# One maximum before the key normalisation in latent attention, the attentions' tables loaded a stage ahead, and unread products in the tails of two expert stages

## The reference

```python
x = x + jnp.tanh(g_xattn[0]) * _L0_xattn_ref(_layernorm(x), ctx, mask, ...)      # 16 heads of 8, mask added
x = x + jnp.tanh(g_ffn[0])   * _L0_ffn_ref(_layernorm(x), ...)                    # ternary weights
x = x + jnp.tanh(g_xattn[1]) * _L1_xattn_ref(_layernorm(x), ctx, ctx, ...)        # 16 heads, relative bias
x = x + jnp.tanh(g_ffn[1])   * _L1_ffn_ref(_layernorm(x), ...)                    # 64 experts, top 3, capacity 64
x = x + jnp.tanh(g_xattn[2]) * _L2_xattn_ref(ctx, _layernorm(x), ...)             # latent attention, below
x = x + jnp.tanh(g_ffn[2])   * _L2_ffn_ref(_layernorm(x), ...)                    # 8 experts, top 2
x = x + jnp.tanh(g_xattn[3]) * _L3_xattn_ref(_layernorm(x), ctx, ...)             # 16 heads, rotated
x = x + jnp.tanh(g_ffn[3])   * _L3_ffn_ref(_layernorm(x), ...)                    # 16 experts, top 2, and a shared one
```

```python
q = (ln @ Wq).reshape(b, m, h, d).transpose(0, 2, 1, 3)
kv = jnp.concatenate([xn @ Wkv, ln @ Wkv], axis=1)
...
qn = rmsnorm(q, qn_g) * scale
kn = rmsnorm(k, kn_g)
sim = jnp.einsum('bhid,bhjd->bhij', qn, kn)
...
attn = jax.nn.softmax(sim.astype(jnp.float32), axis=-1)
out = jnp.einsum('bhij,bhjd->bhid', attn, v)
return out.transpose(0, 2, 1, 3).reshape(b, m, h * d) @ Wout + bout
```

## Time and profile before

| | us |
|---|---|
| median of 3 runs | 1539.1 (1534.62 to 1541.3) |
| profiled execution | 1543.05 |
| its span, first to last instruction | 1541.2 |
| mean granted clock of PE in it | 0.932 |
| busy: PE, DVE, ACT, POOL | 1311.7, 832.4, 690.6, 504.9 |

### The profile page before, as it was taken

The page is one execution under the profiler, slowest core; times in us unless marked ns, Lnnn a source line. Parts: engine busy times, 40 slices in busy tenths (PEclk is TensorE's granted clock), DMA queues, the critical chain, the costliest instruction groups (busy, mean ns, idle before and its releaser), DMA issues. The chain is left out here.

```text
span 1541.2 us, 19784 instructions
## 1 busy us (share of the span) xinstructions
PE 1311.7 (85%) x7007; PEld 570.9 (37%) x7007; DVE 832.4 (54%) x1380; ACT 690.6 (45%) x1158; POOL 504.9 (33%) x479
## 2 busy tenths in 40 slices
PE   5878687649967899999999999999949966677998
PEld 2223232228962333333333333333336752222443
DVE  3767666372335666656665666566274334632554
ACT  3354434422225566656664666465334433353222
POOL 0012301056621555444444455354317750010000
PEclk9899889869987999999999999999979987797999
DMA  8600310149632000000000000000041132000340
GB/s 216 240 1 0 89 39 1 49 156 378 252 84 80 1 1 1 1 0 1 0 1 0 1 1 1 1 1 0 1 146 47 53 91 92 1 1 1 86 95 14
DMA packets 44268, 85.74 MB, mean 56 GB/s; under 512 B 7646, under 2 KB 27230, under 8 KB 43422
## 3 DMA queue, kind: packets, MB, share of 16 engines
q1 hardware_dynamic: 30124, 70.44, 14.3%
q0 software_dynamic: 4544, 9.32, 2.2%
q10 hardware_dynamic: 9504, 4.72, 1.1%
HBM read 76.56 MB, written 11.04 MB: 57 GB/s over the span
## 5 line engine op out<-in xcount | busy, mean ns | idle before, releaser
L2595 ACT ACTIVATE a_prob<-a_TP 128x512 f32<-128x512 f32 x256 | 138.9, 595 | 124.1 <-PE a_TP L2369 122.2
L2726 DVE TENSOR_REDUCE a_lat<-a_SP 128x2 f32<-128x1024 f32 x128 | 156.0, 1218 | 53.0 <-PE a_SP L2335 53.0
L2858 POOL TENSOR_TENSOR a_acc<-a_prob 128x512 f32<-128x512 f32 x64 | 79.8, 1267 | 275.8 <-ACT a_prob L2595 275.8
L2365 PE MATMUL a_TP<-a_qn,a_kn 64*128 64x512 f32 x512 | 148.4, 645 | 2.6 <-ACT a_prob L2595 2.6
L2381 PE MATMUL a_MS<-a_prob,a_V 128*64 128x512 f32 x512 | 123.9, 604 | 0.2 <-ACT a_prob L2595 0.2
L3342 DVE TENSOR_REDUCE a_nm<-a_A 128x8 bf16<-128x616 f32 x84 | 67.0, 797 | 53.4 <-PE a_A L3062 53.3
L3520 POOL TENSOR_TENSOR a_on<-a_osb,a_rden 128x512 f32<-128x512 f32 x9 | 11.4, 1272 | 247.0 <-ACT a_osb L3234 247.0
L2867 POOL TENSOR_TENSOR a_acc<-a_acc,a_prob 128x512 f32<-128x512 f32 x64 | 79.8, 1268 | 18.4 <-ACT a_prob L2595 18.4
L2862 POOL TENSOR_TENSOR a_acc<-a_acc,a_prob 77x512 f32<-77x512 f32 x64 | 80.2, 1273 | 0.0
L2365 PEld LDWEIGHTS a_TP<-a_qn,a_kn 64*128 64x128 f32 x512 | 40.5, 185 | 104.7 <-issue 76.5
L2369 PE MATMUL a_TP<-a_negm,onesb 64*128 64x512 bf16 (+1 forms) x320 | 65.1, 378 | 0.0
(11 more groups left out here) (525 smaller groups left out, 2859.0 us busy)
## 6 DMA issues: line engine op xcount, KB each, us to landing
ring_w<-in_F_w SPq DMA_DIRECT2D x64, 512.0 KB, 8.8
f_wide<-weight_rows SPq DMA_DIRECT2D x24, 256.0 KB, 5.6
a_maskT<-in_maskT SPq DMA_DIRECT2D x1, 2304.0 KB
a_biasT<-in_biasT SPq DMA_DIRECT2D x1, 2304.0 KB
f_b<-in_F_b SPq DMA_DIRECT2D x1, 2048.0 KB
token_rows<-f_xtok ACTq DMA_DIRECT2D x8, 256.0 KB, 7.9
a_biasQ<-in_biasQ SPq DMA_DIRECT2D x3, 616.0 KB, 6.5
ring_w<-expert_rows SPq DMA_DIRECT2D x6, 256.0 KB, 7.1
```

What stands on the lines that cost most here:

```text
L2365: nc.tensor.matmul(TP[0:n, h, :], keys(h), qn[half(h), r % 4, :], start=True, stop=False)
L2595: nc.scalar.activation(prob[0:n, 2 * k + h, :], TP[0:n, h, :], ACT.Exp, bias=rowneg[0:n, b:b + 1] if k == 0 else 0.0).then_inc(p_ready, 1)
L2726: nc.vector.tensor_reduce(lat[:, g % 2, 2 * u:2 * u + 2], SP[:, :, :], AX.X, ALU.max, negate=True).then_inc(s_used, 1)
L2858: nc.gpsimd.tensor_tensor(acc[:, h, :], prob[:, 2 + h, :], prob[:, 4 + h, :], ALU.add).then_inc(added, 1)
```

## The change

Four edits.

1. In `latent_attention`, DVE's `reduce(r + 2, 0)` stands before `norm_k(r + 3)` instead of behind it.
2. The tables of a0, a1 and a3 are placed and loaded by a class `QuadTables` outside the attention: a0's (with the mask) in the block of the shared loads, behind them on SP; a1's weights, vectors and key masks in f0's block; a3's in f2's first block, behind f2's own weights. a1's bias tables are still placed and loaded in a1's block, where they now stand first on SP. What each consumer waits for is unchanged.
3. In f1, 10 products of 128 x 512 that nobody reads are issued on PE behind the last expert product, and one more behind each batch's transposes.
4. In f2 the same with 8 and one for each batch.

```diff
@@ latent_attention, DVE
                     if r + 1 < R:
                         shift(r + 1)
+                    if r + 2 < R:
+                        reduce(r + 2, 0)
                     if r + 3 < R:
                         norm_k(r + 3)
-                    if r + 2 < R:
-                        reduce(r + 2, 0)
                     add_last(r)
@@ load_shared, SP, behind the shared loads
             sp.dma_start(c.ctxrep[:, :, :], d["ctxrep"]).then_inc(loaded, 16)
+            more_loads(sp)
             sp.wait_ge(x_in, 16)
             sp.wait_ge(loaded, 12 * 16)
@@ ternary_ffn
         with nc.Block() as block:
+            @block.sync
+            def _(sp):
+                more_loads(sp)
@@ sorted_glu_moe, PE
                     pe.wait_ge(wide_kept, NT)
                     pe.wait_ge(rest_kept, NT)
+                    def unread(count):
+                        for i in range(count):
+                            nc.tensor.matmul(VP[:, 0, :], c.center[:, :], c.xn[:, 0:S], start=True, stop=True)
+
+                    unread(8)
                     for b in range(B):
                         pe.wait_ge(summed, QT * (b + 1))
...
                         mm.then_inc(back, 1)
+                        unread(1)
@@ capacity_moe, PE
                     down(PAIRS - 1)
+                    unread(10)          # into IDLE, a bank that nothing reads
...
                         mm.then_inc(back, 1)
+                        unread(1)
@@ QuadTables (new), what SP issues
+    def load(self, sp):
+        for dst, src in self.first:
+            sp.dma_start(dst, src).then_inc(self.k_in, 16)
+        for dst, src in self.loads:
+            sp.dma_start(dst, src).then_inc(self.loaded, 16)
+
+    def load_mask(self, sp):
+        self.load(sp)
+        self.load_tall(sp, self.maskT, self.c.dram["maskT"])
+
+    def load_bias(self, sp):
+        for i in range(3):
+            sp.dma_start(self.biasQ[:, i, :], self.c.dram["biasQ"][:, i, :]).then_inc(self.bq_loaded[i], 16)
+        self.load_tall(sp, self.biasT, self.c.dram["biasT"])
@@ flamingo_kernel
+            with ExitStack() as until_first:
+                masked = QuadTables(c, until_first, "a0", "L0_Wq", "L0_Wk", "L0_Wv", mask=True)
+                load_shared(c, masked.load_mask)
+                quad_attention(c, "a0", 0, masked, bv=True, mask=True, more_loads=first_loads(c, ring, ternary))
+            with ExitStack() as until_second:
+                biased = QuadTables(c, until_second, "a1", "L1_Wq", "L1_Wk", "L1_Wv", wo="L1_Wo", relbias=True)
+                ternary_ffn(c, "f0", 4, ternary, biased.load)
+                quad_attention(c, "a1", 1, biased, bv=True, wo=True, relbias=True)
```

More of the change, by code:

```diff
@@ L2011, in _, with unread @@
                             down(n - 1)
+                    def unread(count):
+                        for i in range(count):
+                            nc.tensor.matmul(IDLE[:, :], c.center[:, :], c.xn[:, 0:S], start=True, stop=True)
                     down(PAIRS - 1)
+                    unread(10)
                     for b in range(B):
@@ L2907, in _, with __init__, sb, place_bias @@
                 pool.wait_ge(added, 6 * R)
-def quad_attention(c, name, gate, wq, wk, wv, bq=None, bk=None, bv=None, wo=None, bo=None,
-                   mask=False, relbias=False, rope=False, more_loads=None):
+class QuadTables:
+    def __init__(self, c, ctx, name, wq, wk, wv, wo=None, mask=False, relbias=False, rope=False):
+        self.c = c
+        nc, d = c.nc, c.dram
+        def sb(n, shape, dt=F32):
+            return ctx.enter_context(nc.sbuf_tensor(f"{name}_{n}", shape, dt))
+        self.Wq, self.Wk, self.Wv = sb("Wq", [P, P]), sb("Wk", [P, P]), sb("Wv", [P, P])
+        self.vec = sb("vec", [P, 8])
+        self.first = [(self.Wk[:, :], d[wk]), (self.vec[:, :], d[name + "_vec"])]
+        self.loads = [(self.Wq[:, :], d[wq]), (self.Wv[:, :], d[wv])]
+        if wo:
+            self.Wo = sb("Wo", [P, P])
+            self.loads.append((self.Wo[:, :], d[wo]))
+        if mask:
+            self.maskT = sb("maskT", [P, B * CH, S])
+            self.maskQ = sb("maskQ", [P, B * QT, SK])
+            self.loads.append((self.maskQ[:, :, :], d["maskQ"]))
+        if relbias:
+            self.keym = sb("keym", [P, B * SK], I32)
+            self.rowm = sb("rowm", [P, B * CH], I32)
+            self.first += [(self.keym[:, :], d["keymask"].partition_broadcast(P)),
+                           (self.rowm[0:CR, :], d["rowkeymask"])]
+        if rope:
+            self.Wqp, self.Wkp = sb("Wqp", [P, P]), sb("Wkp", [P, P])
+            self.blk8 = sb("blk8", [P, P])
+            self.qcs = sb("qcs", [P, 2, S])
+            self.kcs = sb("kcs", [P, 2, B * SK])
+            self.first += [(self.Wkp[:, :], d[wk + "_p"]), (self.blk8[:, :], d["blk8"]), (self.kcs[:, :, :], d["kcs"])]
+            self.loads += [(self.Wqp[:, :], d[wq + "_p"]), (self.qcs[:, :, :], d["qcs"])]
+        self.k_in, self.loaded, self.tall_in = (c.sem(f"{name}_{n}") for n in ("k_in", "loaded", "tall_in"))
+        self.bq_loaded = [c.sem(f"{name}_bq_loaded{i}") for i in range(3)] if relbias else []
+    def load(self, sp):
[3 more added lines that the diff above has]
+            sp.dma_start(dst, src).then_inc(self.loaded, 16)
+    def place_bias(self, ctx):
+        self.biasT = ctx.enter_context(self.c.nc.sbuf_tensor("a1_biasT", [P, QUAD * CH, S], F32))
+        self.biasQ = ctx.enter_context(self.c.nc.sbuf_tensor("a1_biasQ", [P, 3, QUAD * ROWS], F32))
+    def load_tall(self, sp, dst, src):
+        even = CR - CR % 16
+        sp.dma_start(dst[0:even, :, :], src[0:even, :, :]).then_inc(self.tall_in, 16)
+        sp.dma_start(dst[even:CR, :, :], src[even:CR, :, :]).then_inc(self.tall_in, 16)
+    def load_mask(self, sp):
[5 more added lines that the diff above has]
+        self.load_tall(sp, self.biasT, self.c.dram["biasT"])
@@ L2914, in quad_attention @@
+def quad_attention(c, name, gate, tables, bv=False, wo=False, mask=False, relbias=False, rope=False,
+                   more_loads=None):
     nc, d = c.nc, c.dram
@@ L2925, in quad_attention @@
         adds = mask or relbias
-        Wq, Wk, Wv = sb("Wq", [P, P]), sb("Wk", [P, P]), sb("Wv", [P, P])
-        vec = sb("vec", [P, 8])
+        Wq, Wk, Wv, vec = tables.Wq, tables.Wk, tables.Wv, tables.vec
+        k_in, loaded, tall_in, bq_loaded = tables.k_in, tables.loaded, tables.tall_in, tables.bq_loaded
+        nfirst, nload = 16 * len(tables.first), 16 * len(tables.loads)
         cv = sb("cv", [P, 6])
@@ L2939, in quad_attention @@
         if wo:
-            Wo = sb("Wo", [P, P])
+            Wo = tables.Wo
         if adds:
@@ L2964, in quad_attention @@
-        bq_loaded = [sem(f"bq_loaded{i}") for i in range(3)]
-        first = [(Wk[:, :], d[wk]), (vec[:, :], d[name + "_vec"])]
-        loads = [(Wq[:, :], d[wq]), (Wv[:, :], d[wv])]
-        if wo:
-            loads.append((Wo[:, :], d[wo]))
-        if mask:
-            loads.append((maskQ[:, :, :], d["maskQ"]))
-        if relbias:
-            first += [(keym[:, :], d["keymask"].partition_broadcast(P)), (rowm[0:CR, :], d["rowkeymask"])]
-        if rope:
-            first += [(Wkp[:, :], d[wk + "_p"]), (blk8[:, :], d["blk8"]), (kcs[:, :, :], d["kcs"])]
-            loads += [(Wqp[:, :], d[wq + "_p"]), (qcs[:, :, :], d["qcs"])]
@@ L2976, in quad_attention @@
-        nfirst, nload = 16 * len(first), 16 * len(loads)
-        EVEN = CR - CR % 16
-        def start_loads(sp):
-            for dst, src in first:
-                sp.dma_start(dst, src).then_inc(k_in, 16)
-            for dst, src in loads:
-                sp.dma_start(dst, src).then_inc(loaded, 16)
-            if relbias:
-                for i in range(3):
-                    sp.dma_start(biasQ[:, i, :], d["biasQ"][:, i, :]).then_inc(bq_loaded[i], 16)
-            if adds:
-                dst, src = (maskT, d["maskT"]) if mask else (biasT, d["biasT"])
-                sp.dma_start(dst[0:EVEN, :, :], src[0:EVEN, :, :]).then_inc(tall_in, 16)
-                sp.dma_start(dst[EVEN:CR, :, :], src[EVEN:CR, :, :]).then_inc(tall_in, 16)
+        bq_cast = sem("bq_cast")
@@ L3016, in quad_attention, with _ @@
         with nc.Block() as block:
-            @block.sync
-            def _(sp):
-                start_loads(sp)
-                if more_loads:
+            if more_loads:
+                @block.sync
+                def _(sp):
                     more_loads(sp)
+            if relbias:
+                @block.sync
+                def _(sp):
+                    tables.load_bias(sp)
             @block.tensor
```

41 lines of the change are left out of this document (16 added, 25 removed).

## The result

The changed kernel took 1517.0 us (median of 4 runs, 1514.3 to 1517.9); the kernel before, measured beside it, 1540.2 (4 runs, 1534.6 to 1544.2). The ratio is 0.9859 with a 95% interval of 0.9838 to 0.9881. The forecast was 1520.5, with a range from 1514 to 1530.

What follows compares the result with a forecast made beforehand. PE was taken to bound latent attention, chains the other stages. Gains of 9.4 + 3.9 + 0.3 + 2.5 + 0.3 + 0.3 + 1.9 = 18.6 us gave 1520.5 us from the median, range 1514 to 1530.

Steps and rivals of the forecast that it cites:

- rival F: Removed pauses keep PE's clock up further into a0, a1 and a3: 22 to 26 us gained, 1515 us; chance 0.07.
- a0's clock: In a0, PE without the mask pause keeps the upper clock through the next stretch: estimated 1.0 us.
- the start of latent attention: Latent attention starts at the upper clock after f1's unread products, ACT's step at about 475.7 instead of 477.61: 1.9 us.
- Step 1: Latent attention's rounds: reduction ahead of key normalisation removes PE's wait for `a_lat`, 29 x 0.325 = 9.4 us.
- Rival C: Latent attention's round is held by `add_last`, stretched 0.89 us: the exchange gives 1.7 us, time 1528.2; chance 0.12.
- Step 2: a0's tables loaded 4.9 us earlier: mask wait of 2.87 us goes and clock stays up, 3.9 us, bounds 1.5 and 5.
- Step 3: a1's tables loaded early: PE's key weight load waits less, 0.3 us, between nothing and 1.2.
- Step 4: a3's tables loaded early: key product sooner, 2.5 us at the upper clock, 0.65 at the lower.
- Steps 5 and 6: Unread products in f1's and f2's tails: about 0.3 us in each tail, and 1.9 at latent attention's start.
- Rival B: Clock does not hold through f1's and f2's tails: 1527.4 us with both lost, 1524 with one; chance 0.28.

## Why the prediction was right, and where it was not

The time lies in the stated range, but the forecast gain was 18.6 us and the measured one 23.2. At 1517.0 us it stands at the very edge of the forecast's own range (1517 to 1524), and inside the 22 to 26 us of rival F. That it came this near is in part luck: two terms were too small or missing (a0's clock, the end of latent attention), and one was too large over all kernels (the start of latent attention).

The lengths of all profiled executions, by what a kernel has:

| stretch | without | with | difference |
|---|---|---|---|
| a2's rounds, the exchange | 545.92 to 545.96 (5) | 536.04 to 536.49 (7) | -9.5 |
| a0, early tables | 103.95 to 107.58, mean 106.2 (4) | 98.66 to 99.89, mean 99.5 (6) | -6.8 |
| a1, early tables | 116.11 to 122.46, mean 119.0 (5) | 118.96 to 119.48, mean 119.1 (6) | none |
| a2's start, unread in f1 | 69.09 to 70.93, mean 69.8 (5) | 68.17 to 70.76, mean 69.0 (8) | -0.8 |
| a3, tables and unread in f2 | 126.13 to 129.09, mean 127.4 (4) | 121.08 to 127.06, mean 124.4 (5) | -3.0 |
| a2's end | 30.84 to 30.87 (3), 28.38 (1) | 28.37 to 28.39 (8, all with the exchange) | -2.5 mostly |

Left out are the kernels whose own edit lies in the stretch: unread products inside or at the end of a0, a1 and a3, the lengthened rounds, and in the last row's "without" the kernel with the filled last round. With the two that have unread products at a3's end the mean of a3 would be 124.8. The two ranges of a3 overlap, so its 3.0 us are less sure than the key product's move.

**Step 1, right.** 9.4 us were forecast, 9.5 came, and the exchange alone gives them. The reasoning held in its parts: L2358 0.21 us behind the product before it, `cast_k` behind `norm_k`, no wait at `sums`; inside a batch the turns stand 17.10 to 17.11 us apart, before 17.43 to 17.44. One part of it was off: `add_last` did not stay at 1.28 us. It was stretched by 0.41, inside the bound of 0.6 that the length of `cast_k` gave, and that left 0.2 us at `sums` in the place of 0.63. Rival C was right about the mechanism and wrong about the size, and the lengthened round shows how near it was: 0.6 us more on DVE cost 0.50 in each round. The Trainium skill (SBUF — State Buffer, Who interferes with whom) says that a VectorE instruction with two inputs in SBUF contends with a GpSimd instruction that reads SBUF, and calls the port pair between them an exclusive lock. The trace agrees in kind: beside each other the two additions and the cast last from 782.37 to 784.06, 1.69 us, where their own lengths add up to 1.89.

**Step 2, the step that failed, by size.** The mechanism stood (the mask's wait gone, `ctxrep` not late), and the forecast of 3.9 us was mis-sized: 6.8 by the means, 7.3 in the pair. The failed term is the clock, taken as 1.0 us. DVE's row shows the parts, cut at the mask's conversion and at the first shift (the first copy of `a_negm`), in the same four and six kernels as in the table:

| a0, us | without early tables (4) | with (6) | difference of the means | pause filled, mask late |
|---|---|---|---|---|
| stage's start to the conversion | 20.98 to 22.09 | 18.19 to 19.37 | 2.6 | 21.47 |
| conversion to first shift | 9.04 to 9.76 | 7.56 | 1.8 | 7.57 |
| first shift to the stage's end | 73.10 to 76.86 | 72.90 to 72.96 | 2.3 | 73.00 |

So 2.6 us were the wait and about 4 the clock, since the kernel with the pause filled has only the wait left. The estimate priced one stretch at half rate, from rows at 36 to 38, and took a part of that off again as DVE's: 1.0 us where 1.8 came. It did not look at 48 to 60, where the clock was down a second time: 0.72 in the kernel before, 0.50 in two others with a late mask. That second dip does not follow the pause every time. In the kernel with the filled last round DVE waited 3.56 us for the mask, and the clock was

```profile
48.00:60.00 12.00, 10.15 (x88) 3.26 (x92) 9.38 (x11) 4.61 (x5) 0.00 (x0) 1.00 0.99 396
```

with a0 at 103.95 us; what decides it stays open. Nor is the changed kernel free of a dip, only of the long ones: its clock was 0.66 at 42 to 47. In the pair, 0.9 of the 7.3 us are chance: the key table (DVE's `a_kexp`) came 5.79 us behind the stage's start instead of 6.72, and over all kernels it comes at 5.75 to 6.96, whatever the tables.

**Step 3, nothing that can be measured.** The pair shows 1.5 us, but a1 without early tables ranges from 116.1 to 122.5 us. The expected move of the cast came about in neither kernel of the pair: it takes 1.69 us in both.

**Step 4, right, by both edits.** 2.5 forecast, 3.0 by the means, 2.5 in the pair. The prediction gave 0.65 for the tables alone, and 0.4 to 0.8 came; with the unread products alone nothing that can be told.

**Steps 5 and 6, right at the place, less in the sum.** ACT's step of the earlier trace rows stands 3.07 us behind the stage's start instead of 4.85, and the stage took 2.0 us less to its first turn in the pair, as forecast. Over all kernels it is 0.8, since in both kinds the clock falls again later in that stretch, for a longer or a shorter time. The clock did hold: it was 0.72 at 450 to 455 in f1's tail and back at 1.00 before the stage began, and in each of the eight kernels with these products the first one of the stage took 1.10 us. Rival B did not occur. The tails themselves, from the last expert product to the next stage, took 23.51 us instead of 24.17 in f1 and 18.54 instead of 18.58 in f2, where 0.3 us were forecast for each.

**What the sum had left out.** The end of latent attention, 2.5 us, was not foreseen. There PE has pauses of 0.68 and 0.48 us in the last round, and behind them the clock dips in the kernel before and does not in the changed one. The four score products behind the second pause, first before, then after (there the fourth stands on a row of its own, and the four end at 1078.97, 1.61 us from their start):

```profile
1099.16 2.56 PE L2365 MATMUL a_TP<-a_qn,a_kn 64*128 64x512 f32 x4 [0.48 <-ACT a_prob L2595]
```

```profile
1077.36 1.18 PE L2388 MATMUL a_TP<-a_qn,a_kn 64*128 64x512 f32 x3 [0.48 <-ACT a_prob L2618]
...
1078.38 0.59 PE L2388 MATMUL a_TP<-a_qn,a_kn 64*128 64x512 f32 x1
```

None of the eight kernels with the exchange had the dip (two of them had the pauses filled as well), and three of four without it had. As one without the exchange escaped too, and as filling the pauses removed it, it is a matter of the clock's moment and not of the exchange as such; why the exchange avoids it each time stays open. Most of these 2.5 us did not last. In the changed kernel the clock dips a little later, in f2's head (0.66 in its first 5 us), whose first centring products take longer than before, first before, then after:

```profile
1120.52 1.96 PE L702 MATMUL f_CEN<-xT,center 128*128 128x512 f32 x4 [2.10 <-PEq L57]
```

```profile
1096.22 2.67 PE L712 MATMUL f_CEN<-xT,center 128*128 128x512 f32 x4 [2.09 <-PEq L57]
```

L731 stands 18.20 us behind f2's start there instead of 16.73, so 1.5 us went back, which more than accounts for the 0.8 us by which f2 is longer in the pair. Of the 13 profiled kernels three had the dip in the last round of latent attention, five in f2's head (two of them without the exchange), and five in neither place.

The lengths of the pair add up to 9.5 + 7.3 + 2.5 + 2.5 + 2.0 and 2.3 of small ones, its 26.1 us. The medians differ by 23.2, because the profiled execution before, 1543.05 us, lay 2.85 over its median and the one after at its own. Rival F (more than forecast, by the clock) was thus nearer to what happened than its chance of 0.07.

## What to carry to other kernels

Where two engines hang on each other and PE goes idle, price the pause twice: once as the wait, and once as the work behind it at the lower clock, over the whole chain that follows, and look for a second dip further on. An early load and a clock that is kept up can each be worth little alone and pay together, since the later of the two sets the time. When an operation is moved beside one on another engine, read the slack that it leaves from the trace afterwards, even if the total is unchanged: here 0.63 us had become 0.2, and an added operation of 0.68 us cost 0.50.

## What was not expected of the hardware

The same program on the same kind of chip loses its clock at different places: a0, unchanged in four kernels, took 103.95 to 107.58 us, and a1 without early tables 116.11 to 122.46, with no instruction different in them. The rounds of latent attention, at the upper clock throughout, repeat to 0.04 us in 546 in the five kernels with the old order. The Trainium skill (TensorE: Matmul & The Clock Gate, Part 1: The HAM clock gate) says that the moment of the clock's change varies from run to run of one kernel; these traces agree: in three profiles of the changed kernel L731 stands 18.20, 16.73 and 18.20 us behind f2's start. A stage of a few hundred us with pauses can thus not be judged by one pair of profiles.

An unread product is cheap only where it fills a pause: of the two in a0 the first, inside its pause, moved nothing, and the second, behind its pause and at the lower clock, took 2.00 us and pushed the scores by 1.9.
